# The last three blocks get buffers of their own, and the last weights' pieces are made on chip

## The reference

```
x = x + einsum(layernorm(x), weight * mask)           # 2048 tokens, 1024 wide, mask in 32x32 blocks
l = layernorm(x) @ W_gate + b_gate                     # 8 experts
y[e] = relu(layernorm(x) @ W_e[e] + b_e[e])            # 1024 -> 1024
out = x + mean of y over the two experts with the largest l
```

## Time and profile before

| | us |
|---|---|
| median of 3 runs | 657.02 |
| the three runs | 654.74, 657.02, 670.6 |
| profiled execution, its own time | 654.89 |
| its span, first to last instruction | 653.2 |
| PE busy | 626.7 (96%) |
| DVE busy | 356.3 (55%) |
| ACT busy | 355.4 (54%) |
| POOL busy | 273.0 (42%) |

### The profile page before, as it was taken

One profiled execution on the slowest core, in us unless ns is written; L12 is line 12 of the kernel. 1 busy time (PEld: TensorE's weight loads), 2 busy tenths in 40 slices (PEclk: granted clock), 3 DMA queues, 4 the chain that ended last, 5 costly groups with the idle time before them and its releaser, 6 DMA issues.

```text
span 653.2 us, 11366 instructions
## 1 busy us (share of the span) xinstructions
PE 626.7 (96%) x3495; PEld 507.9 (78%) x3498; DVE 356.3 (55%) x639; ACT 355.4 (54%) x434; POOL 273.0 (42%) x252
## 2 busy tenths in 40 slices
PE   6999999999999999999999999999999999999971
PEld 5666777888888888888888888888888878778861
DVE  5896597877877666245245253045233324589051
ACT  7777763867775733453543445354354644554561
POOL 2013213223655347556353535446353444646413
PEclk9999999999999999999999999999999999999985
DMA  8991874699864469969689689659999999898510
GB/s 346 407 407 66 341 272 161 221 335 315 293 252 164 162 208 242 260 206 240 159 230 257 140 226 271 133 158 257 212 188 303 196 217 290 199 207 172 91 36 2
DMA packets 90360, 144.45 MB, mean 221 GB/s; under 512 B 58432, under 2 KB 58432, under 8 KB 90304
## 3 DMA queue, kind: packets, MB, share of 16 engines
q1 hardware_dynamic: 26928, 97.04, 41.1%
q0 software_dynamic: 11376, 33.57, 23.6%
q10 hardware_dynamic: 52000, 13.11, 11.8%
HBM read 91.79 MB, written 46.14 MB: 211 GB/s over the span
## 4 chain that ended last, share of the span: by engine, by line
PE 87%; ACTq 5%; ACT 3%; DMA 2%; issue 1%; SPq 0%; POOLq 0%; POOL 0%; DVE 0%
PE psO L561 76%; ACTq L1196 4%; PE psT L851 2%; PE psT L561 2%; PE psT L594 2%; ACT x2T L1204 2%; PE psO L594 1%; PE psG L667 1%; DMA xb<-data_t 1%; ACT xb L1251 1%; DMA rows_out<-xb,tok_of 1%; PE psS L648 1%; ACTq L1235 0%; PE psT L635 0%; ACTq L1234 0%
## 5 line engine op out<-in xcount | busy, mean ns | idle before, releaser
L561 PE MATMUL psO<-slots,xT 128*128 (+1 forms) x1728 | 397.8, 391 | 2.4 <-ACT psO L1149 2.3
L561 PEld LDWEIGHTS psO<-slots,xT 128*128 128x128 f32 x1728 | 322.7, 188 | 70.5 <-issue 4.1
L1543 DVE CAST slots<-raw 128x1024 fp32r<-128x1024 f32 x56 | 50.6, 903 | 190.2 <-DMA raw<-L_ffn_W_e 100.9
L561 PE MATMUL psO<-wT,xT 128*128 128x512 f32 x624 | 152.3, 397 | 0.0
L1251 ACT ACTIVATE xb<-psO 128x512 f32<-128x512 f32 x78 | 46.5, 596 | 172.0 <-PE psO L561 123.1
L1963 POOL DMA_INDIRECT rows_out<-xb,tok_of x36 | 65.2, 1811 | 172.4 <-ACT xb L1251 158.5
L561 PEld LDWEIGHTS psO<-wT,xT 128*128 128x128 f32 x624 | 114.3, 188 | 25.1 <-issue 2.7
L1957 POOL TENSOR_TENSOR xT<-x2T,xT 128x1024 fp32r<-128x1024 f32 x35 | 88.4, 2525 | 25.2 <-ACT xT L1212 14.5
L1545 DVE TENSOR_TENSOR slots<-raw,slots 128x1024 fp32r<-128x1024 f32 x56 | 75.0, 1340 | 1.9
L1149 ACT ACTIVATE psO<-bias_slot 128x512 f32 (+1 forms) x78 | 47.0, 602 | 39.0 <-issue 17.2
L1883 POOL TENSOR_SCALAR rs<-squares 128x1 f32<-128x1 f32 x16 | 7.8, 486 | 69.8 <-ACT rows_a L998 40.6
(11 more groups left out here) (284 smaller groups left out, 613.2 us busy)
## 6 DMA issues: line engine op xcount, KB each, us to landing
raw<-L_ffn_W_e SPq DMA_DIRECT2D x64, 512.0 KB, 5.5
x_rows<-x SPq DMA_DIRECT2D x16, 512.0 KB, 4.5
xb<-data_t SPq DMA_DIRECT2D x12, 512.0 KB, 4.6
mask_stage<-mask_blocks SPq DMA_DIRECT2D x8, 512.0 KB, 10.9
w_stage<-weight_t SPq DMA_DIRECT2D x8, 512.0 KB, 11.6
row_stage<-L_attn_weight SPq DMA_DIRECT2D x8, 512.0 KB, 10.9
xr<-L_attn_data SPq DMA_DIRECT2D x8, 512.0 KB, 6.7
x_planes<-planes_even SPq DMA_DIRECT2D x8, 512.0 KB, 3.2
```

The lines of the kernel that those rows point to most:

```text
L561: last = eng.matmul(psum, xT[:, p, a, kt, :], moving(b, kt), start=(i == 0 and kt == 0 and not seeded), stop=(i == len(PASSES) - 1 and kt ...
L1543: eng.tensor_copy(slots[:, e % 2, HI, kt, :], raw[:, kt % 2, :]).then_inc(c_split, 1)
```

## The change

The eighth matrix is not loaded again. DVE makes `w3` from the high and low parts in `slots[1]`: cast the high part to the first piece, subtract it, **add the low part** (new), cast to the second piece, subtract to the third. So there are five operations for each part instead of four, and no wait for a load. DVE starts when `pace` says that `slots[0]` is free, and waits no second time.

`x3` has three places of its own: two behind `w3` in `slots[0]`, one over `xT`. The rows of block 37 are joined in a spare row buffer, those of 36 and 38 in `x2T`. Blocks 36 and 37 get accumulators in `psT`, which PE's transposes no longer use by then; block 38 stays in `psO`. Result rows of 37 and 38 go to `raw`.

ACT's order for block 35 is written out: join 36, start the transpose of 38, join 37, relu(35, 0), join 38, seed both halves of 36, relu(35, 1), seed 37, seed 38, and then the six relus of the last blocks. POOL adds block 35 in two halves, waits until both have landed, and starts the adds of 36, 37 and 38, each after its own relus, with no wait between them. PE's transposes are written as matmuls in transpose mode that set the `start` flag only at the first of each four. In the core of the diff (`flat` merges the last two axes, `add_halves` is the former `add_last_rows` for block b, `l_tail` are three new semaphores, and SP waits for them at the end):

```diff
@@ -95,7 +96,8 @@
         xb = sb("xb", [P, 2, D], F32)
         xr_offset = cursor[0]
         xr = sb("xr", [P, 2, D], F32)
-        x3 = at("x3", [P, 2, 4, KT, P], BF16, cursor[0])
+        x3 = [at("x3_0", [P, 3, KT, P], BF16, slot_base + 6 * KT * H), at("x3_1", [P, 3, KT, P], BF16, slot_base + 6 * KT * H + 6 * D),
+              at("x3_2", [P, 3, KT, P], BF16, cursor[0])]
...
+        spare_rows = [(rows_a[:], rows_b[:], x2[:, 0, :])[(SPARE_RING + i) % 3] for i in (1, 2)]
+
+        def joined_rows(b):
+            return spare_rows[1] if b == SURE + 1 else flat(x2T[:])
+
+        def out_rows(b):
+            return xb[:, b % 2, :] if b <= SURE else raw[:, LAST - b, :]
+
+        def result(b, n):
+            return psO[:, n, :] if b in (LAST, SURE - 1) else acc(b - SURE + 1, n)
...
-                if place < N_EXP:
-                    load_bias(place, expert)
+                load_bias(place, expert)
 
             for p in range(2):
-                added = (N_BLOCKS - 1 - p) // 2 + 1
-                if p == LAST % 2:
+                added = (SURE - 1 - p) // 2 + 1
+                if p == (SURE - 1) % 2:
                     added += NH - 1
                 eng.wait_ge(l_add[p], 16 * added)
+            for tail in l_tail:
...
                 for kt in range(KT):
-                    last = eng.transpose(psT[:, turn_bank(b), kt, :], rows_of(b, slice(kt * P, (kt + 1) * P)), ident[:])
+                    place = psT[:, turn_bank(b), kt, :]
+                    rows = rows_of(b, slice(kt * P, (kt + 1) * P))
+                    last = eng.matmul(place, rows, ident[:], start=kt % (KT // 2) == 0, stop=True, is_transpose=True,
+                                      skip_group_check=True)
                 last.then_inc(c_t1 if b == 0 else c_turn, 1)
...
                 piece_x, piece_w = TERMS[i]
                 width = eng.shape_register(0)
                 for kt in range(KT):
-                    last = eng.matmul(psO[:, n, :].shape_from_register(width), x3[:, b % 2, piece_x, kt, :],
+                    last = eng.matmul(result(b, n).shape_from_register(width), x3[b - SURE][:, piece_x, kt, :],
                                       w3[:, piece_w, kt, n * HALF:(n + 1) * HALF].shape_from_register(width),
                                       start=False, stop=(i == len(TERMS) - 1 and kt == KT - 1), skip_group_check=True)
                 return last
...
-            eng.wait_ge(c_w3, W3 * KT)
+            eng.wait_ge(c_w3, W3_OPS * KT)
             for b in range(SURE, N_BLOCKS):
...
             def join_rows(b):
                 eng.wait_ge(*landed(b))
-                if b <= SURE:
-                    eng.wait_ge(c_rlo, b - 1)
-                else:
-                    eng.wait_ge(c_x3, X3 * (b - SURE - 1) + X3_TAKEN)
-                joined = eng.activation(x2T[:].bitcast(U16).rearrange("p k (t h) -> p h (k t)", h=2),
+                eng.wait_ge(c_rlo, min(b, SURE) - 1)
+                if b == SURE + 1:
+                    eng.wait_ge(c_turn, turns_of_pe(TAIL))
+                elif b == LAST:
+                    eng.wait_ge(c_x3, X3_TAKEN)
+                joined = eng.activation(joined_rows(b).bitcast(U16).rearrange("p (x h) -> p h x", h=2),
                                         turned_by(b).rearrange("p (h k) t -> p h (k t)", h=2), ACT.Copy)
                 if b >= SURE:
                     joined.then_inc(c_rhi, 2)
...
-            for b in range(N_BLOCKS):
-                if 1 < b + 1 < N_BLOCKS and b != 1 and not by_dma(b + 1):
+            def relu(b, n):
+                eng.wait_ge(c_half, NH * (b + 1) + n + 1)
+                eng.activation(out_rows(b)[:, n * HALF:(n + 1) * HALF], result(b, n) if b >= SURE else psO[:, n, :], ACT.Relu,
+                               scale=1.0 / TOP_K).then_inc(c_out, 1)
+
+            def seed_last(b, n):
+                eng.activation(result(b, n), bias_slot[:, (N_EXP - 1) % 2, n * HALF:(n + 1) * HALF], ACT.Copy).then_inc(c_seed, 1)
+
+            for b in range(SURE - 1):
+                if b + 1 > 1 and b != 1 and not by_dma(b + 1):
                     rows_hi(b + 1)
-                if b + 1 < N_BLOCKS and by_dma(b + 1):
+                if by_dma(b + 1):
                     join_rows(b + 1)
                 if b >= 2:
                     eng.wait_ge(l_add[b % 2], 16 * (b // 2))
                 for n in range(NH):
-                    eng.wait_ge(c_half, NH * (b + 1) + n + 1)
-                    eng.activation(xb[:, b % 2, n * HALF:(n + 1) * HALF], psO[:, n, :], ACT.Relu,
-                                   scale=1.0 / TOP_K).then_inc(c_out, 1)
-                    if b + 1 < N_BLOCKS:
-                        if n == 0:
-                            slot = biases_of(b + 1)
-                        seed_half(b + 1, slot, n)
+                    relu(b, n)
+                    if n == 0:
+                        slot = biases_of(b + 1)
+                    seed_half(b + 1, slot, n)
                     if n == 0 and b + 3 < N_BLOCKS and by_dma(b + 3):
                         turn_rows(b + 3)
                     if b == 1 and n == 0:
                         rows_hi(b + 1)
+
+            b = SURE - 1
+            join_rows(SURE)
+            turn_rows(LAST)
+            join_rows(SURE + 1)
+            eng.wait_ge(l_add[b % 2], 16 * (b // 2))
+            relu(b, 0)
+            join_rows(LAST)
+            eng.wait_ge(c_split, 2 * KT * N_EXP)
+            for n in range(NH):
+                seed_last(SURE, n)
+            relu(b, 1)
+            for n in range(NH):
+                seed_last(SURE + 1, n)
+            eng.wait_ge(c_out, NH * (b + 1))
+            for n in range(NH):
+                seed_last(LAST, n)
+            eng.wait_ge(l_add[SURE % 2], 16 * (SURE // 2))
+            for b in range(SURE, N_BLOCKS):
+                for n in range(NH):
+                    relu(b, n)
...
+            when = pace[0:1, 0, N_EXP - 2:N_EXP - 1]
+            used = eng.value_load(when, min_val=NH, max_val=NH * (N_BLOCKS + 1))
+            eng.wait_ge(c_half, used)
+            eng.wait_ge(c_split, 2 * KT * N_EXP)
             for kt in range(KT):
                 chunk = raw[:, kt % 2, :]
-                if kt % 2 == 0:
-                    when = pace[0:1, kt // 2, N_EXP - 2:N_EXP - 1]
-                    used = eng.value_load(when, min_val=NH, max_val=NH * (N_BLOCKS + 1))
-                    eng.wait_ge(c_half, used)
-                eng.wait_ge(l_raw[kt % 2], 16 * ((KT * (N_EXP - 1) + kt) // 2 + 1))
-                eng.tensor_copy(w3[:, 0, kt, :], chunk).then_inc(c_w3, 1)
-                eng.wait_ge(c_w3, W3 * kt + 1)
-                eng.tensor_tensor(chunk, chunk, w3[:, 0, kt, :], ALU.subtract).then_inc(c_w3, 1)
-                eng.wait_ge(c_w3, W3 * kt + 2)
+                high, low = (slots[:, (N_EXP - 1) % 2, part, kt, :].bitcast(F32) for part in (HI, LO))
+                done = W3_OPS * kt
+                if kt >= 2:
+                    eng.wait_ge(c_w3, done - W3_OPS)
+                eng.tensor_copy(w3[:, 0, kt, :], high).then_inc(c_w3, 1)
+                eng.wait_ge(c_w3, done + 1)
+                eng.tensor_tensor(chunk, high, w3[:, 0, kt, :], ALU.subtract).then_inc(c_w3, 1)
+                eng.wait_ge(c_w3, done + 2)
+                eng.tensor_tensor(chunk, chunk, low, ALU.add).then_inc(c_w3, 1)
+                eng.wait_ge(c_w3, done + 3)
                 eng.tensor_copy(w3[:, 1, kt, :], chunk).then_inc(c_w3, 1)
-                eng.wait_ge(c_w3, W3 * kt + 3)
+                eng.wait_ge(c_w3, done + 4)
                 eng.tensor_tensor(w3[:, 2, kt, :], chunk, w3[:, 1, kt, :], ALU.subtract).then_inc(c_w3, 1)
-            rest_rows = (rows_a[:], rows_b[:], x2[:, 0, :])[(SPARE_RING + 1) % 3]
+
+            rest_rows = spare_rows[0]
             eng.wait_ge(c_turn, turns_of_pe(TAIL))
+            eng.wait_ge(c_half, NH * (SURE - 1))
             for b in range(SURE, N_BLOCKS):
                 done = X3 * (b - SURE)
+                piece_1, piece_2, piece_3 = (flat(x3[b - SURE][:, piece, :, :]) for piece in range(3))
                 eng.wait_ge(c_rhi, 2 * b)
-                eng.wait_ge(c_half, NH * b)
-                eng.tensor_copy(x3[:, b % 2, 0, :, :], x2T[:]).then_inc(c_x3, 1)
+                if b == LAST:
+                    eng.wait_ge(c_half, NH * SURE)
+                eng.tensor_copy(piece_1, joined_rows(b)).then_inc(c_x3, 1)
                 eng.wait_ge(c_x3, done + 1)
-                eng.tensor_tensor(rest_rows, x2T[:].rearrange("p k t -> p (k t)"), x3[:, b % 2, 0, :, :].rearrange("p k t -> p (k t)"),
-                                  ALU.subtract).then_inc(c_x3, 1)
+                eng.tensor_tensor(rest_rows, joined_rows(b), piece_1, ALU.subtract).then_inc(c_x3, 1)
                 eng.wait_ge(c_x3, done + 2)
-                eng.tensor_copy(x3[:, b % 2, 1, :, :].rearrange("p k t -> p (k t)"), rest_rows).then_inc(c_x3, 1)
+                eng.tensor_copy(piece_2, rest_rows).then_inc(c_x3, 1)
```

(49 more changed lines are left out.)

## The result

| | us |
|---|---|
| changed kernel, median of 4 runs | 646.43 (645.89 to 646.64) |
| kernel before, median of 4 runs | 655.88 (653.61 to 670.6) |
| ratio, with its 95% interval | 0.9866 (0.9832 to 0.9900) |
| profiled execution, its own time and span | 645.89 and 644.2 |

Some executions run at a lower granted clock and take some per cent longer, like the one at 670.6 us; ratios, and the medians of the table of experiments, leave these out. About 9 us, 1.3%: faster by more than the interval and less than 2%. The forecast was 647.0 with a span of 644.3.

What follows compares the result with a forecast made beforehand. PE's fp32 matmuls were taken to bound the kernel, followed by a 26 us tail of waits. Gains of 7.7 + 1.2 = 8.9 us off the 653.2 span gave 644.3, own time 646.0, forecast 647.0 us; range 643.5 to 652.5.

Steps and rivals of the forecast that it cites:

- parts 1 to 3: Tail after block 35: ACT's new order, PE's three blocks in a row and POOL's adds without landing waits together gain 7.7 us.
- 4.3 "in any case": End of the span: 4.3 us follow the last add's landing, whatever else changes.
- The adds' share: POOL's last adds: no wait for block 37's landing and no second half's start, 3.4 of the 7.7 us.
- part 4: DVE's weight pieces from 560 us: forty operations with 10 us of stretching end at 612 and cost nothing.
- part 5: PE from 560 to 603 us: without eight second loads, two waits for seeds vanish, gaining 1.2 us (ends 0 and 1.2).
- rival E: Dropping the loads gives nothing; both PE gaps from 560 to 603 us stay, time 648.2 us; chance 0.16.
- part 6: PE's transposes at L851: same operation with other flags, no change; 1.3 us if each were slower by a tenth.
- A: Tail gains half: block 38's transpose and an add land late, 5.1 of 7.7 us gone, 651 to 652 us; chance 0.2.
- B: ACT's single queue holds the last relus, so PE's earlier end is worth nothing; 650.5 to 651.5 or 655 us; chance 0.12.
- C: DVE's weight pieces end late, at 631.7 us, because POOL's work blocks DVE; slower, 656 to 660 us; chance 0.04.
- D: More than the sum: transpose's start 1.36 us, halves without a gap, median beside the profile; 644 to 645 us; chance 0.12.
- The added half of the difference to the median: Whole time: profiled execution lay 2.1 us below the runs' median; half of that was added, giving 647.0 us.

Runs made afterwards that it cites:

- Adds only: Kernel before, with block 38 added by one indirect DMA that waits for no landing, in place of two halves; median 653.72 us, ratio to before 0.9984.
- seeds first, whole: Changed kernel with the four seeds of blocks 36 and 37 ahead of the last transpose's start, and block 35 added by one DMA; median 645.73 us.
- two more operations: Changed kernel with one subtraction done twice more for each of the eight weight parts; median 658.00 us, ratio to before 1.0056.
- seeds first: Changed kernel with the four seeds of blocks 36 and 37 moved ahead of the last transpose's start on ACT; median 645.88 us, ratio to before 0.9856.
- changed again: The changed kernel run once more with nothing altered; median 647.62 us, ratio to before 0.9865.
- one more operation: Changed kernel with one subtraction done once more for each of the eight weight parts; median 646.81 us.

## Why the prediction was right

**The tail, parts 1 to 3.** Predicted 7.7 us, measured 7.65 in the first execution and 7.4 in the second (0.16 less if both ends of block 35 are the modelled ones). Against the second execution of the kernel before, whose tail was 25.8 us, it is 7.1 and 6.8. By its points: the walk had PE start block 36 1.3 us after block 35, it was 0.88, and 1.38 in the second execution; PE took 9.0 us for three blocks against 8.9; the relu ended 10.51 us after block 35 against 10.85. POOL then took 1.23 us to start and not 0.84. From there 6.96 us to the end of the span, forecast as 7.0. Two terms of that sum, 2.7 us to the landing and then 4.3 "in any case", came out here, but the reading behind the second is wrong. The runs show that what comes last is POOL's drain, at no fixed distance from the landing. Adds only is where that reading fails: 3.45 us at the add's start gave 2.2 at the end. That the changed kernel has the drain of the kernel before, and not one 1.3 us longer, is luck.

**The adds' share.** Predicted 3.4 of 7.7 us for the landing no longer waited for. Taken off alone it brings 2.2 us; put back into the changed kernel it costs 4.6. It is larger there because the relus come early enough for the whole row of adds to be exposed, and because the half's start took 1.2 us behind the landing where 0.8 was expected; and 2.2 is low by the longer drain of 1.3 us. So 3.4 lies between the two, and neither run has exactly that share.

**The pieces on chip, part 4.** Predicted end 612, measured 609.36, and 615.00 in the second execution, which started 2.3 us later; cost nothing, as predicted. The stretching was 7.8 us and then 11.1, around the 10 of the forecast. In the first execution four of the forty operations carry it, each beside one of POOL's subtractions, as here at 577 us (DVE, then POOL):

```profile
577.32 2.88 DVE L1863 CAST w<-slots 128x1024 bf16<-128x1024 f32 x1
```

```profile
577.08 2.57 POOL L2010 TENSOR_TENSOR xT<-x2T,xT 128x1024 fp32r<-128x1024 f32 x1
```

Three of the four are casts with one input (2.77 to 2.88 us against 0.69). In the second execution five are stretched, all with two inputs (3.29 to 3.79 us against 1.23). So it is the operation that happens to meet POOL's that stretches, of either kind. The rule of the Trainium skill, SBUF — State Buffer (Who interferes with whom), that I cited was the one on two inputs, and the second execution agrees with it. The same section has copies and casts among the operations that can take the shared ports as well, and the three casts of the first execution agree with that.

**Eight loads less, part 5.** Predicted 1.2 us, within a bound of 0 to 1.2; the runs give 0.5 on average, so this term was mis-sized. The comparison of the first two traces showed 1.35 us ahead of the tail, and that looked like a confirmation. It is not: 2.45 us of idle time after 500 us became 0.76, part of it at 531 us, where both kernels do the same, and the next execution of the changed kernel ended block 35 later than before did. The mechanism (loads in flight lengthen the transposes' starts) is shown; rival E's number, 0, was as near as mine. The lock rule of the Trainium skill, Perfetto Trace Analysis (DMA Instruction — HWDGE), lets a load hold ACT for no more than its own start, 0.33 us here, and by it alone no start of 5.4 us comes out of one of 2.9; so the trace goes beyond that rule.

**The transposes, part 6.** No change, as predicted. One line before and after, columns ns min/median/max:

```profile
L851 PE MATMUL psT<-ident,rows_a x40: 270/272/273, 210.6 to 437.1; 128*128 128x128 f32 x40
```

```profile
L869 PE MATMUL psT<-ident,rows_a x40: 270/272/273, 210.0 to 437.3; 128*128 128x128 f32 x40
```

**The rivals.** A did not come in the changed kernel, but its second half did in three variants, where block 35's landing took 5.1 to 5.4 us. B (ACT's one queue eats the gain) is wrong: the last relu came 4.7 us nearer to block 35. C's bounds (some cost from a chain end of 626.85, a loss from about 629) lie inside what the two runs bracket, 621.35 and 631.8. D has its first condition, a transpose's start of 1.34 us and not 1.98, and its last, a median beside the profile; the halves did not follow without a gap, and no run of the changed kernel was as low as its 644 to 645. The added half of the difference to the median was right by luck: the first four runs lay at 646.4, the next four that count at 647.6.

## What to carry to other kernels

Measure a tail from one event on the engine that bounds the rest, not from the start of the span; here that takes out 5 us of scatter. A chain of short dependent steps is shortened only if each shared thing in it goes at once, buffers, accumulators and landings: alone, the adds brought 2 us and the order 3. Count how much cover a hidden chain has left behind which engine's next work, for the first thing it delays is not the consumer but the queue in between.

## What the runs showed of the hardware

- An indirect DMA that moves nothing mostly lands 2.7 to 3.6 us after its start, but 5.1 to 5.4 for block 35's second half in three variants and 4.0 to 5.1 for block 37's add with the old tail; a real add of 128 rows with idle engines took 6.0.
- POOL's closing drain ends 5.1 to 5.2 us after the end of its last DMA instruction in most kernels, 6.4 to 6.5 in two (adds only; seeds first, whole), 7.7 with the real add, and takes 6.3 us with nothing in flight. What it waits for was not found.
- In the tail, where PE is busy for 8.1 of 18.7 us after a long stretch without idle time, TensorE's granted clock falls from 1.00 to 0.50 (from 2.4 to 1.2 GHz). The 96 matmuls of 16 columns of an empty block hardly show it: 2.56 us at 0.97 in the changed kernel (block 36), 2.73 us at 0.50 with two more operations.
- The same program ended block 35 at 625.5 and 628.0 us in two executions, and the ones that differ from it only later between 624.9 and 630.2.

**POOL's DMA starts beside VectorE.** Part of the late landings is VectorE. The instruction on POOL takes 1.55 us, but when it starts while a DVE operation on the row pieces runs, it is longer by nearly what is left of that operation, in all such cases after 626 us but one. Block 37's add in the kernel before started at 638.54 and took 2.55 us; it started 1.12 us before the end of this operation:

```profile
638.44 1.22 DVE L1834 TENSOR_TENSOR x<-rows_a,x 128x1024 bf16<-128x1024 f32 x1
```

With 0.38, 0.52 and 0.98 us left (seeds first, changed again, one more operation) block 35's second half took 1.80, 1.93 and 2.41 us. Its landing moved by the same in four executions: 2.9, 3.0, 3.1 and 3.2 us behind instructions of 1.73, 1.86, 1.93 and 2.05. The late landings of the first point above have a further 0.8 to 2.2 us, which stay open: in the kernel before, block 37's packets ran 3.2 us after its start, and the landing came 2 us behind them.
